# A sandwich block of attention and NF4 feed-forward on one core: fp32 transposes of the V block written as plain matmuls with the identity

## What is computed

```python
x = x + _layernorm(_L0_attn_ref(_layernorm(x), Wq, Wk, Wv, Wo))       # 16 heads of 64, causal, rotary
x = x + _layernorm(_L0_ffn_ref(_layernorm(x), gate..., up..., down...))  # NF4 codes, 1024 x 2752

# inside the attention
q = (hidden_states @ Wq).reshape(b, s, HEADS, HEAD_DIM)
k = (hidden_states @ Wk).reshape(b, s, HEADS, HEAD_DIM)
v = (hidden_states @ Wv).reshape(b, s, HEADS, HEAD_DIM)
```

## Time and profile before

| | us |
|---|---|
| median of 3 runs | 3297.59 |
| lowest and highest | 3293.02, 3301.31 |
| profiled execution, its own time | 3296.03 |
| its span | 3294.2 |
| PE busy in the span | 2897.0 (88%) |
| DVE busy | 2390.9 (73%) |
| ACT busy | 2022.5 (61%) |

### The profile page before, as it was taken

How to read it: one execution, slowest core, us unless ns; L and a number is a source line. 1 busy time by engine, 2 the same in 40 slices (tenths; PEclk the granted TensorE clock), 3 DMA queues, 4 the chain that set the end, 5 groups by cost and what they waited for, 6 DMA issues and landing times. The chain is left out here.

```text
span 3294.2 us, 58839 instructions
## 1 busy us (share of the span) xinstructions
PE 2897.0 (88%) x17856; PEld 1547.4 (47%) x17856; DVE 2390.9 (73%) x4289; ACT 2022.5 (61%) x4003; POOL 121.6 (4%) x397
## 2 busy tenths in 40 slices
PE   4989999688888888985883699999999999999996
PEld 2534444466666666663441244444444444444442
DVE  6535555688888888884556787787777777777767
ACT  1114443688888888882214767676676676676742
POOL 0000000000000000000002000000000000000002
PEclk9999999899999999997996899999999999999998
DMA  4322222201010101102112111111111111111124
GB/s 164 116 77 58 76 76 64 72 22 40 22 41 22 40 22 35 27 5 86 64 70 69 53 52 49 50 52 52 46 52 49 50 52 45 53 46 52 52 71 153
DMA packets 77773, 188.88 MB, mean 57 GB/s; under 512 B 12304, under 2 KB 12688, under 8 KB 77200
## 3 DMA queue, kind: packets, MB, share of 16 engines
q1 hardware_dynamic: 77456, 185.13, 17.7%
HBM read 151.52 MB, written 33.55 MB: 56 GB/s over the span
## 5 line engine op out<-in xcount | busy, mean ns | idle before, releaser
L1234 PE MATMUL gp<-region,wgu 128*128 128x512 f16 x4224 | 931.3, 383 | 89.3 <-DVE wgu L1392 89.3
L1271 ACT ACTIVATE line<-code,offsets 128x512 f32<-128x512 f32 x1056 | 697.2, 713 | 111.3 <-DVE below L1370 45.7
L1234 PEld LDWEIGHTS gp<-region,wgu 128*128 128x128 f16 x4224 | 416.0, 99 | 600.9 <-issue 110.9
L786 ACT ACTIVATE probs<-logits,nbias,coef 128x512 f32<-128x512 f32 (+3 forms) x640 | 461.0, 720 | 100.4 <-POOL nbias L719 86.4
L1247 PE MATMUL yp<-wd,inter 128*128 128x512 f16 x2112 | 463.9, 380 | 24.5 <-DVE wd L1392 17.4
L835 DVE SCALAR_TENSOR_TENSOR pt_pair<-tp,pt_pair 128x512 f16<-128x512 f32 (+3 forms) x640 | 385.8, 603 | 76.2 <-ACT pt_pair L795 72.4
L736 PE MATMUL logits<-k_sb,q_sb 128*128 128x512 f16 (+3 forms) x1280 | 347.3, 354 | 104.6 <-ACT probs L786 61.2
L819 DVE TENSOR_REDUCE mx<-logits 128x1 f32<-128x512 f32 (+3 forms) x640 | 383.9, 600 | 33.7 <-PE logits L736 33.1
L795 ACT ACTIVATE pt_pair<-tp 128x512 f16<-128x512 f32 (+3 forms) x640 | 343.4, 537 | 25.2 <-PE tp L749 21.0
L749 PE MATMUL tp<-ident,probs 128*128 128x128 f32 x2176 | 349.2, 276 | 4.3 <-DVE pt_pair L835 2.7
L548 PE MATMUL pq<-region,wt_pair 128*128 128x512 f16 x1536 | 333.4, 380 | 14.9 <-DVE wt_pair L599 14.9
(11 more groups left out here) (107 smaller groups left out, 2823.0 us busy)
## 6 DMA issues: line engine op xcount, KB each, us to landing
qk_pairs<-r_pair SPq DMA_DIRECT2D x128, 128.0 KB, 2.1
k_sb<-qk_pairs SPq DMA_DIRECT2D x64, 256.0 KB, 5.4
cst<-in_gate_codes SPq DMA_DIRECT2D x44, 256.0 KB, 2.6
sst<-in_gate_scales SPq DMA_DIRECT2D x88, 128.0 KB, 2.9
cst<-in_up_codes SPq DMA_DIRECT2D x44, 256.0 KB, 2.7
sst<-in_up_scales SPq DMA_DIRECT2D x88, 128.0 KB, 3.1
cst<-in_down_codes SPq DMA_DIRECT2D x44, 256.0 KB, 2.7
sst<-in_down_scales SPq DMA_DIRECT2D x88, 128.0 KB, 3.0
```

Source lines behind the costliest of these rows:

```text
L786: a.activation(probs[:, g0 % P_RING, 0:w * P], sp_[:, g0 % S_RING, 0:w * P], ACT.Exp, bias=nbias[:, m:m + 1], scale=col(coef, 0), accum_ou ...
L1234: mm = pe.matmul(gp[:, e % 2, m, :], wgu[:, par, m, a, col0:col0 + P], xnT[:, b, k, tok], start=(k == 0 and a == b), stop=(k == KT - 1 and ...
L1271: a.activation(line[:, k % 4, :], code7[:, :], ACT.Identity, scale=slope, bias=offsets[:, k:k + 1]).then_inc(s_L.sem, 1)
```

## The change

The call that writes a transposed piece into PSUM is `pe.transpose` before and `pe.matmul` with `start=True, stop=True` after, with the same three operands. The product of the piece, read as the stationary operand, with the identity is the piece transposed, too. Only the V block has the change; the other transposes stay. The number, the order and the waits of the calls are the same on every engine. In the built program each of these calls is one weight load and one matmul before, and two of each after (over the whole program, loops not unrolled, 4544 of each before and 4576 after: 32 calls are written out in the V block).

```diff
@@ -361,7 +361,7 @@
                     pe.wait_ge(s_h.sem, s_h.done(i))
                     pe.wait_ge(s_tlo.sem, s_tlo.room(i))
                     for k in range(KT):
-                        mm = pe.transpose(tp[:, u, k, :], ht[:, u, k * P:(k + 1) * P], ident[:, :])
+                        mm = pe.matmul(tp[:, u, k, :], ht[:, u, k * P:(k + 1) * P], ident[:, :], start=True, stop=True)
                     mm.then_inc(s_T1.sem, 1)
```

## The result

The changed kernel is slower: its median is 3313.5 us (3310.3 to 3318.2, 4 runs) against 3296.6 us for the kernel before (3293.0 to 3301.3, 4 runs), a ratio of 1.0056 with a 95% interval of 1.0044 to 1.0068. That is +16.9 us by the medians, and 14.5 to 22.4 us by the interval. The forecast was 3310; its range began at 3302 and took in the 3323 of the open weight loads. The profiled execution took 3315.5 us.

The account below looks back on a forecast made before the run. PE, full in the V block from 45.94 us, was taken as the bound: 15 sets x 0.87 = 13.1 us on 3296.0 or 3297.6 gave 3309.1 and 3310.7, said as 3310. The 8-in-10 range went down to 3302 and took in 3323.

Parts of the forecast that it names:

- the open weight loads: Rival, V block: second load not hidden beside the first matmul; 0.215 us more a product, 25.8 us, 3323; chance 0.13.
- What bounds the block: V block: PE never waits from 45.94 us until the last projection ends, so work added to PE adds to the block.
- Two matmuls, each at a transpose's pace: V block: each plain product is two pairs at 0.109 us, 0.218 us, 0.109 more; 15 sets of 8 give 13.1 us.
- The Trainium skill's four passes: V block: a true fp32 product takes four high and low part passes of 128 columns, estimated 0.213 us a product.
- four times today's transpose: Rival, V block: a product costs 0.436 us, 0.327 more, 39.2 us in all, 3336; chance 0.09.
- The two halves share the work: Rival, V block: each of a product's two matmuls streams once at 0.06 us; 1.3 us in all, 3299; chance 0.08.
- Set 1 and the clock: V block, second 8 transposes: grow 1.76 us at the low clock, 0.88 us net if the clock rises when it did.
- The early rise: Rival, V block start: longer PE work brings the high clock sooner, at most 2.8 us back, 3307; chance 0.10.
- The later stages only move: After the V block: same program moved by 13 us, stages as long as before, 3 us allowed each way for the clock.

Follow-up runs that it names:

- set 0 alone: Plain products only in the V block's first 8 transposes, the other 15 groups left as in the kernel before: 3296.1 us, ratio 0.9997.
- the halves: Each plain product of the changed kernel's V block cut into two of 64 moving columns: 3344.6 us, ratio 1.0146 against the kernel before.
- set 0 doubled: Kernel before with each of the V block's first 8 transposes issued twice, in transpose mode: 3296.9 us, one execution, no ratio.

## Why the prediction was right, and where it was not

- **What bounds the block** was right. PE is full from the second set on, and nothing in the loop takes up the added work: 14 turns of +0.911 us are 12.8 us, and set 0 alone costs nothing.
- **Two matmuls, each at a transpose's pace** was right in size. 0.109 us more were said, 0.114 measured; transposes issued twice took 0.874 of the 0.911 us a turn. The term was 13.1 for 15 sets; with 0.114 it is 13.7. The reason given for it, that the load stays hidden behind the stream, is not borne out: the halves show that something beside the stream, probably the load, takes 0.11 us a pair, just as long as the stream. That it added almost nothing was luck. The rival "loads come into the open" looked at the right thing, but took 0.053 us for a load and laid it behind the stream; if it is the load, it is twice as long and runs beside the stream, and the whole excess over a transpose is 3 ns. The Trainium skill's four passes (FP8 and Floating Point Precision, TensorE Precision Notes), for which the forecast had an estimate of 0.213 us, fit the 0.224 us that a product takes. The Trainium skill's statement that transpose mode is four times faster for FP32 (TensorE: Matmul & The Clock Gate, Terms), read as four times today's transpose, gave 0.436 us, which does not fit.
- **The two halves share the work**, the rival on the other side: excluded; a pair takes 0.11 us and not 0.06.
- **Set 1 and the clock.** The early rise, given one chance in ten, came in both profiles of the changed kernel. From the first matmul to the start of the third set it was 16.70 and 16.60 us against 18.28 and 16.90, so it gives back 0.2 to 1.7 us. The forecast had 0.9 us added there. The rise came early after a longer first set, once in transpose mode as well, though not always, and chance is not excluded. The rule that transposes do not count for the full clock (the Trainium skill, TensorE: Matmul & The Clock Gate, Part 4: PE-mode transpose) is not borne out: in the run with set 0 doubled PE had done 16 transposes and nothing else when the clock rose.
- **The later stages only move** was the step that failed: "all stages after it as long as before". They were set at 0, 3 us each way. Attention's own span did stay, 882.2 us before and 882.5 after. The tail alone took 4.2 us (25.5 and 25.7 against 21.1 and 21.6), the border ahead of the output stage about 1.2 (29.4 and 29.6 against 28.5 and 28.1). The long tail goes with a packet of the instruction queue at one place in all 14 profiles, and adding matmuls to PE's program moved both, in both kernels. How so small a transfer costs 4 us was not shown.

Together: 12.8 for the turns, less 0.2 to 1.7 for the start, plus 4.2 for the tail and about 1.2 for the border, is 16.5 to 18.0; measured 16.9. The V block itself came to 11.1 to 12.6 of the 13.1 us that were forecast. The forecast of 13 held because its range was wide enough, not because it had the other 5 us; that part was luck.

## What to carry to other kernels

An fp32 transpose written as a plain product costs twice a transpose on PE, 0.224 us against 0.109 for a 128 x 128 tile; it is paid in full where PE is the bound and to about 60% where it was 88% busy. Cutting the moving side smaller does not help: a pair with 64 moving columns takes 0.110 us, hardly less than the 0.112 of one with 128, and a product then needs twice as many. Before a difference under 0.2% is put down to what an edit computes, add the same number of instructions in a place where they are free: here a longer program alone made the kernel 0.1% slower, and with 10 matmuls more than that the difference could not be told from none, though part of the delay had only moved ahead of the last matmul.

## What the runs showed of the hardware that was not expected

- The pairs of a plain fp32 product follow each other every 0.110 us with 64 moving columns and every 0.112 us with 128. The weight load, recorded with 192 ns, is the likely limit of the short ones. In transpose mode it is recorded with 140 ns, and transposes of 128 columns follow each other every 0.109 us.
- PE can be busy without a pause and stay at the low clock: in the one profile with them, 64 pairs of such loads and 64-column matmuls ran for 13.7 us at 0.214 us a pair.
- Transposes alone can come before the rise of the clock: after 16 of them, 8 more ran in 1.09 us instead of 1.97.
- With one 16 KB packet of instructions among back-to-back row transfers a 21 us tail was 4 us longer; with the packet 8 us earlier PE waited 2.5 us longer for its last matmuls instead. That it belongs to PE's program is inferred from its moving with that program's length; the trace does not name the engine. Which part of the delay is the shared DMA engines and which the order of SyncE's waits was not tried.
